# First attention's keys projected two heads at once and doubled by transfers within SBUF, the experts' gate kept in PSUM, the second sequence loaded later, in a kernel of two decoder blocks

## What is computed

```
# block 0, attention: 8 heads of 64; keys and values from the 512 tokens and 77 context rows
q = ln @ Wq ; k, v = split(concat([ctx_norm, ln]) @ Wkv)      # 589 keys
attn = softmax(8 * q @ k.T) ; x = x + tanh(g) * (attn @ v) @ Wout
# block 0, feed-forward: activations in 8 bit steps, ternary weights
h = silu(depthwise_conv1d(bit_linear(norm(x), w1))) ; x = x + tanh(g) * bit_linear(h, w2)
# block 1, attention: 16 heads of 8 against the 77 context rows, rotary positions
# block 1, feed-forward: 8 experts of 64, 2 chosen, and one shared expert
s = softmax(x @ gate_w.T) ; y = sum over chosen e of s_e * (silu(x @ wg_e) * (x @ wu_e)) @ wd_e
```

## Time and profile before

| | before |
|---|---|
| median of three runs | 289.64 us (289.44 to 291.3) |
| profiled execution: its time, its span | 291.28 us, 289.3 us |
| TensorE busy | 265.5 us, 92% |
| VectorE busy | 230.0 us, 79% |
| ScalarE busy | 172.6 us, 60% |
| GpSimd busy | 40.6 us, 14% |
| granted TensorE clock, mean share of full speed | 0.994 |

### The profile page before, as it was taken

One profiled execution on the slowest core, in us unless ns is written; L12 is line 12 of the kernel. 1 busy time (PEld: TensorE's weight loads), 2 busy tenths in 40 slices (PEclk: granted clock), 3 DMA queues, 4 the chain that ended last, 5 costly groups with the idle time before them and its releaser, 6 DMA issues.

```text
span 289.3 us, 5593 instructions
## 1 busy us (share of the span) xinstructions
PE 265.5 (92%) x1918; PEld 198.5 (69%) x1918; DVE 230.0 (79%) x545; ACT 172.6 (60%) x344; POOL 40.6 (14%) x60
## 2 busy tenths in 40 slices
PE   0999999999999999988899999999989868889796
PEld 0757877788789875667666678777657755575565
DVE  3698768796679998999898989758789989885751
ACT  1378856576775678587576659664357622752152
POOL 2200000000010000103100001003532030000650
PEclk9999999999999999999999999999999999999899
DMA  7950000000000000000000000000000100000001
GB/s 198 345 184 3 0 1 2 0 2 0 2 1 3 0 0 2 0 3 0 0 3 0 2 2 1 2 0 2 1 11 0 29 0 0 2 2 1 0 2 36
DMA packets 5856, 6.13 MB, mean 21 GB/s; under 512 B 555, under 2 KB 4805, under 8 KB 5829
## 3 DMA queue, kind: packets, MB, share of 16 engines
q1 hardware_dynamic: 4944, 4.66, 5.2%
q10 hardware_dynamic: 885, 1.12, 1.1%
HBM read 5.26 MB, written 0.52 MB: 20 GB/s over the span
## 4 chain that ended last, share of the span: by engine, by line
PE 68%; DVE 15%; issue 9%; ACT 4%; DMA 1%; POOL 1%; DVEq 0%; ACTq 0%; POOLq 0%
PE slot L510 19%; PE slot L583 12%; PE slot L564 6%; PE slot L565 5%; PE slot L555 3%; PE slot L556 3%; PE slot L548 2%; PE slot L542 2%; PE slot L677 2%; DVE mx L1095 2%; PE slot L590 2%; PE slot L643 2%; PE slot L655 2%; PE slot L726 1%; PE slot L660 1%
## 5 line engine op out<-in xcount | busy, mean ns | idle before, releaser
L804 ACT ACTIVATE PR<-slot,nm 128x589 f32<-128x589 f32 x64 | 47.5, 749 | 22.2 <-DVE nm L992 21.9
L992 DVE TENSOR_REDUCE nm<-slot 128x1 f32<-128x589 f32 x64 | 46.2, 762 | 4.2 <-PE slot L565 4.0
L510 PE MATMUL slot<-K,PR 128*128 128x128 f32 (+1 forms) x320 | 43.1, 276 | 0.4 <-ACT PR L804 0.4
L510 PEld LDWEIGHTS slot<-K,PR 128*128 128x128 f32 (+1 forms) x320 | 35.9, 142 | 8.1 <-ACT PR L804 4.4
L564 PE MATMUL slot<-KH,Q 128*128 128x296 f32 (+1 forms) x128 | 40.2, 332 | 0.1
L583 PE MATMUL slot<-PT,V 128*64 128x256 f32 (+1 forms) x320 | 38.1, 384 | 0.0
L565 PE MATMUL slot<-KL,Q 128*128 128x296 f32 (+1 forms) x128 | 36.1, 299 | 0.0
L741 ACT ACTIVATE PT<-slot 128x640 f32<-128x640 f32 x39 | 26.8, 704 | 12.6 <-PE slot L510 12.2
L583 PEld LDWEIGHTS slot<-PT,V 128*64 128x64 f32 (+1 forms) x320 | 21.6, 137 | 11.9 <-issue 2.7
L564 PEld LDWEIGHTS slot<-KH,Q 128*128 128x128 f32 x128 | 24.1, 189 | 3.5 <-issue 1.7
L565 PEld LDWEIGHTS slot<-KL,Q 128*128 128x128 f32 x128 | 24.2, 189 | 0.5 <-issue 0.5
(11 more groups left out here) (163 smaller groups left out, 516.2 us busy)
## 6 DMA issues: line engine op xcount, KB each, us to landing
CTT<-in_ctxT SPq DMA_DIRECT2D x1, 640.0 KB, 8.3
K<-in_const ACTq DMA_DIRECT2D x1, 589.0 KB, 8.9
WGU<-in_wgu SPq DMA_DIRECT2D x1, 580.0 KB, 8.5
X<-in_x SPq DMA_DIRECT2D x2, 256.0 KB, 3.9
WK<-in_wk SPq DMA_DIRECT2D x1, 512.0 KB, 6.5
out<-X SPq DMA_DIRECT2D x8, 64.0 KB, 1.5
L1W<-in_l1w SPq DMA_DIRECT2D x1, 384.0 KB, 8.4
WD<-in_wdT SPq DMA_DIRECT2D x1, 320.0 KB, 9.7
```

Source lines behind the costliest of these rows:

```text
L510: return pe.transpose(dst, src, ident[0:p, 0:p])
L804: act.activation(PR[:, s, :], W[:, K0:K0 + KEYS0], ACT.Exp, bias=nm0[:, s:s + 1], accum_out=sum0[:, b, p * 2 + f, t, e:e + 1]).then_inc(pr ...
L992: dve.tensor_reduce(nm0[:, s:s + 1], W[:, K0:K0 + KEYS0], AX.X, ALU.max, negate=True).then_inc(max_ready, 1)
```

## The change

1. A `k` item now holds a **pair** of heads: 8 items instead of 16, with the same two matmuls each. The product has one head on rows 0 to 63 and the other on rows 64 to 127. ScalarE and VectorE write `KH` and `KL` in two instructions of 64 rows each. SyncE then copies each 64 rows to the other half of the rows, four transfers for a pair (151 KB each), and a score item waits for `k_doubled`. `WK` is half as large (256 KB instead of 512): of each pair's four copies of 64 columns the two middle ones are loaded.
2. The experts' gate: ScalarE writes the tanh to PSUM, over the up product that it had copied; VectorE computes `(tanh + 1) * HM` once GpSimd has multiplied `HM`, and in an added stage `D2` multiplies by the gate product in PSUM. GpSimd's second multiplication (L503) is gone, and with it the waits that came of `HB` sharing memory with `TH`. The bank is held one stage longer.
3. The second half of `x` is loaded after `WK` and `WV`; its statistics and normalisation become stages of `x0` with places in the plan.
4. The plan is another one: other banks and another interleaving. More copies go to ScalarE: of the 64 copies behind `u` 45 instead of 39, of the 8 behind `f3` 7 instead of 4.

```diff
-        out += [("k", b, h) for h in range(H0)]
+        out += [("k", b, p) for p in range(NP0)]
...
 PLAN = """
-x0:F0 x0:A1 k:F2+8@2 k:F4 x0:D2 k:A1 k:F0 k:A1 k:D1 q:F6 k:D1 k:A1 q:F7 s:D2 q:A1 v:F2 k:D1 q:A1 q:D1 v:F4
+x0:F0 x0:A1 k:F2+8@2 x0:D2 q:F4 k:A1 v:F0 q:A1 s:D2 x0:P2 k:F6 v:Ca k:D1 q:F5 k:A1 q:D1 q:F0 q:A1 v:F2 k:D1
...
-        WK = sb("WK", [P, H0, P])
+        WK = sb("WK", [P, NP0, P])
...
+        k_doubled = [sem(f"k_doubled{i}") for i in range(2)]
...
-                    "m3": (shared_ready, n), "m2": (hid_ready, n), "m4": (y_ready, n)}[item[0]]
+                    "m3": (shared_ready, n), "m2": (hidw_ready, n), "m4": (y_ready, n)}[item[0]]
...
-            for b in range(B):
-                sp.dma_start(X[:, b * QT:(b + 1) * QT, :], xv[:, b * QT:(b + 1) * QT, :]).then_inc(ld[f"x{b}"], 16)
-            sp.dma_start(WK[:], wk.rearrange("p (h c) -> p h c", h=H0)).then_inc(ld["wk"], 16)
+            sp.dma_start(X[:, 0:QT, :], xv[:, 0:QT, :]).then_inc(ld["x0"], 16)
+
+            pairs = wk.rearrange("p (q c) -> p q c", q=NP0)[:, :, DH0:DH0 + P]
+            sp.dma_start(WK[:], pairs).then_inc(ld["wk"], 16)
             sp.dma_start(WV[:], wv).then_inc(ld["wv"], 16)
+            sp.dma_start(X[:, QT:, :], xv[:, QT:, :]).then_inc(ld["x1"], 16)
...
+            for g in range(B * NP0):
+                for part, signal in ((KH, k_upper), (KL, k_ready)):
+                    sp.wait_ge(signal, 2 * (g + 1))
+                    for e in range(2):
+                        r, o = slice(e * DH0, (e + 1) * DH0), slice((1 - e) * DH0, (2 - e) * DH0)
+                        s = (2 * g + e) % 4
+                        sp.dma_start(part[o, s, :].bitcast(F32), part[r, s, :].bitcast(F32)).then_inc(k_doubled[g % 2], 16)
...
-                    pe.wait_ge(k_ready, g + 1)
+                    pe.wait_ge(k_doubled[g // 2 % 2], 64 * (g // 4 + 1))
...
-                    act.activation(KH[:, g % 4, :], W[:, K0:K0 + KEVEN], ACT.Copy).then_inc(k_upper, 1)
+                    for e in range(2):
+                        r = slice(e * DH0, (e + 1) * DH0)
+                        act.activation(KH[r, (2 * g + e) % 4, :], W[r, K0:K0 + KEVEN], ACT.Copy).then_inc(k_upper, 1)
...
-                    dve.tensor_tensor(KL[:, (n - 1) % 4, :], W[:, K0:K0 + KEVEN], KH[:, (n - 1) % 4, :].bitcast(F32),
-                                      ALU.subtract).then_inc(k_ready, 1)
+                    for e in range(2):
+                        dve.wait_ge(k_upper, 2 * n - 1 + e)
+                        r, s = slice(e * DH0, (e + 1) * DH0), (2 * (n - 1) + e) % 4
+                        dve.tensor_tensor(KL[r, s, :], W[r, K0:K0 + KEVEN], KH[r, s, :].bitcast(F32),
+                                          ALU.subtract).then_inc(k_ready, 1)
...
-                    act.activation(HB[:, (n - 1) % 2, :], slot(item)[:, 0:MH], ACT.Tanh, scale=0.5).then_inc(gate_tanh, 1)
+                    act.wait_ge(up_copied, n)
+                    act.activation(W[:, MH:2 * MH], W[:, 0:MH], ACT.Tanh, scale=0.5).then_inc(gate_tanh, 1)
...
-                    hb = HB[:, (n - 1) % 2, :]
-                    dve.scalar_tensor_tensor(out=hb, in0=hb, scalar=1.0, in1=W[:, 0:MH],
+                    dve.wait_ge(upw_ready, n)
+                    hm = HM[:, (n - 1) % QT, 0:MH]
+                    dve.scalar_tensor_tensor(out=hm, in0=W[:, MH:2 * MH], scalar=1.0, in1=hm,
                                              op0=ALU.add, op1=ALU.mult).then_inc(hid_ready, 1)
...
+                elif kind == "m2":
+                    dve.wait_ge(hid_ready, n)
+                    hm = HM[:, (n - 1) % QT, 0:MH]
+                    dve.tensor_tensor(hm, hm, W[:, 0:MH], ALU.mult).then_inc(hidw_ready, 1)
```

More of the change, by code:

```diff
@@ L154, in takes @@
     kind, n = item[0], item[-1]
-    return {"x0 D2": n == 0, "f4 P2": n % TP == TP - 1, "f4 D3": n % TP == TP - 1}.get(f"{kind} {stage}", True)
+    return {"x0 D2": n == 1, "x0 P2": n == 1, "x0 D3": n == 1, "f4 P2": n % TP == TP - 1, "f4 D3": n % TP == TP - 1}.get(f"{kind} {stage}", True)
 def orders():
@@ L249, in mega_kernel @@
         rt = sb("rt", [P, NT, 4])
[L250 removed]
+        hot = sb("hot", [P, TP, 2, E1])
         cwt = sb("cwt", [P, NT, E1])
@@ L494, in power @@
                 n = upto(item)
-                rstd(*{"n": (1, n - 1, PARTS), "f4": (2, n // TP - 1, PARTS), "a6": (3, n - 1, PARTS)}[item[0]])
-            def halves(item):
-                n = upto(item)
-                pool.wait_ge(hid_ready, n)
-                pool.wait_ge(upw_ready, n)
-                hm = HM[:, (n - 1) % QT, 0:MH]
-                pool.tensor_tensor(hm, hm, HB[:, (n - 1) % 2, :], ALU.mult).then_inc(hidw_ready, 1)
-            walk("POOL", {"P1": work, "P2": power, "P3": halves})
+                rstd(*{"x0": (0, 1), "n": (1, n - 1, PARTS), "f4": (2, n // TP - 1, PARTS), "a6": (3, n - 1, PARTS)}[item[0]])
+            walk("POOL", {"P1": work, "P2": power})
         @block.tensor
@@ L549, in front @@
                 elif kind == "k":
-                    h = item[2]
+                    p = item[2]
                     pe.wait_ge(lt_ready, 2 * (b + 1))
@@ L960, in _ @@
                                   ALU.subtract, ALU.mult).then_inc(cn_ready, 1)
-            dve.wait_ge(ld["x1"], 16)
-            all_stats(0, X, slice(QT, NT))
-            variance(0, slice(QT, NT), twice=True)
             def early(item):
@@ L1129, in second @@
                 if kind == "x0":
-                    dve.wait_ge(rstd_ready[0], 2)
-                    for m in range(QT, NT):
-                        normalise(0, X, m, XN[:, m, :], xn_ready[0])
-                    dve.wait_ge(ld["ident"], 16)
-                    dve.tensor_copy(identb[:], ident).then_inc(identb_ready, 1)
+                    dve.wait_ge(ld["x1"], 16)
+                    all_stats(0, X, slice(QT, NT))
+                    variance(0, slice(QT, NT), twice=True)
                 elif kind == "s":
@@ L1200, in third @@
                 kind, n = item[0], upto(item)
-                if kind == "n":
+                if kind == "x0":
+                    dve.wait_ge(rstd_ready[0], 2)
+                    for m in range(QT, NT):
+                        normalise(0, X, m, XN[:, m, :], xn_ready[0])
+                    dve.wait_ge(ld["ident"], 16)
+                    dve.tensor_copy(identb[:], ident).then_inc(identb_ready, 1)
+                elif kind == "n":
                     dve.wait_ge(rstd_ready[1], n)
```

116 lines of the change are left out of this document (52 added, 64 removed).

## The result

The changed kernel takes 286.76 us (median of four runs, 285.93 to 287.35) against 289.54 for the one before (289.05 to 291.3): a ratio of 0.9891, 95% interval 0.9843 to 0.994. It is faster by 1.1%, which is clear of the noise; I had forecast 283, 2.3%, so it is 3.8 us short of the forecast. The profiled execution took 286.67 us, its span is 284.9.

What follows compares the result with a forecast made beforehand. TensorE was taken to bound the first 40 scores, VectorE the next 16, no engine the later chains. Stretches 21.4 + 81.7 + 56.5 + 105 + 18.5 = 283.1 us, plus 2.0 less 1.6: 283.5, written 283; own range 279 to 287, with rivals 276 to 291.

Steps and rivals of the forecast that it cites:

- TensorE bounds it, so TensorE work taken out of B is time: First to 40th score maximum: TensorE busy 82.8 of 83.2 us, so less TensorE work there shortens the kernel.
- B: Stretch from the first to the 40th score maximum; forecast 81.7 us for 83.2, at least 79.5.
- The first doubling's queue: Pair 1's key transfers wait behind SyncE's loads, ending about 18 us; landing at about 20, at worst 21 us.
- A: Start to the first score maximum: loads, first normalisation and projections; forecast 21.4 us for 20.5, at most 22.5.
- Rival 3: Doublings late, a pair's last transfer over 5 us from a loaded queue; +3 to +4 us, time 287; chance 0.10.
- −1.6: Final step: median of three runs lay 1.64 us below the profiled execution, so 1.6 us is subtracted.
- E: Last normalised rows to the end, the last experts; forecast 18.5 us for 17.2, range 16.5 to 20.
- D: 64th score maximum to last normalised rows; forecast 105 us for 75.4, VectorE busy 94.5 us times ratio 1.11.
- Rival 1: VectorE stays fed behind the last score, ratio 1.087, and TensorE's cut shows in full; time 276; chance 0.15.
- C: Stretch from the 40th to the 64th score maximum; forecast 56.5 us for 93.0, range 54 to 60.
- Load of the second sequence: At the start, moving this load from the queue's head gains nothing, since the first sequence's chain never waited behind it.
- Normalisations under 400 ns: Sign in the changed profile: the normalisations' mean, 452 ns before, falls under 400 ns with fewer GpSimd multiplications.

Runs made afterwards that it cites:

- e18: Kernel before, old order, with four more filling transposes ahead of each of the sixteen key items, 64 in all; 295.84 us, ratio 1.0197.
- e5: e1's kernel with nine filling transposes ahead of each of the eight key items, putting the key products' time back; 293.4 us, ratio 1.0066.
- e9: Kernel before, old order, with the eight odd heads' key products in bfloat16, rougher output; 290.75 us, ratio 1.0003.
- e13: e8's kernel with all eight pairs' key products in bfloat16, rougher output; 281.49 us, ratio 0.9702.
- e17: e8's kernel with maxima over every second column and key products in bfloat16, only times used; 277.75 us, ratio 0.9554.
- e16: e8's kernel with each score's maximum over every second column and exponential's scale 0.8, another output; 280.22 us, ratio 0.9635.
- e2: Kernel before, old order, with the key part alone (pairs of heads, doubling by transfers); 304.47 us, ratio 1.0445.
- e12: e2's kernel with the five late loads moved behind the first two pairs' doublings; 298.47 us, ratio 1.0281.
- e8: e1's kernel with fourteen more filling transposes behind the second a6 item's back stage; 282.13 us, ratio 0.9741.
- e1: Changed kernel with five late weight loads issued behind the transfers that double the first two pairs of keys; 284.45 us, ratio 0.9809.
- e15: e8's kernel with each pair's two steps of doublings held back on SyncE by a small load and its wait; 287.2 us, ratio 0.9911.
- e4: Changed kernel with GpSimd's second multiplication back in place of VectorE's added stage; 289.41 us, ratio 0.9975.
- e11: Changed kernel with only the fourteen filling transposes behind the second a6 item, loads where they were; 284.25 us, ratio 0.9798.
- e6: e1's kernel with the third pair's query copy on ScalarE placed behind the three exponentials of its group; 287.72 us, ratio 0.9914.
- e7: e1's kernel with 7 of the 28 ScalarE copies behind the first 40 scores given back to VectorE; 284.32 us, ratio 0.9867.
- e10: e8's kernel with the second half of x loaded ahead of the key and value weights again; 281.95 us, ratio 0.9711.

## Why the prediction was wrong

- **"TensorE bounds it, so TensorE work taken out of B is time": the step that failed.** It was read from 82.8 busy of 83.2 us. A full engine shows that more of its work will cost (e18 6.3 of 6.7 us, e5 7.5 of 7.5), not that less will gain (between the 1st and the 64th maximum: e9 nothing of 3.4 us, e13 0.4 of 4.3, or 1.1 without its fallen clock, e17 beside e16 1.5 of 4.3). The key part alone lengthens the old order by 15 us, 9 with the queue out of the way (e2, e12). Yet in the new order putting the key time back costs 7.6 us, e5 against e8: 288.4 us of span against 280.8. With its key time put back the new order (288.4) is no better than the old one (287.3 at full clock). So in these runs neither the order nor the saved time gains by itself; only the new plan together with the saved time does. B's term was 4.0 us too small: 0.8 of it more busy time, 3.2 idle. My sum had taken 1.5 us of items off B's old length one for one, as if the new order would leave TensorE as little idle as the old one (0.4 us); it idles 3.6, of which 2.3 are for ScalarE's exponentials and 1.2 for copies by VectorE and ScalarE.
- **The first doubling's queue was named, and mis-sized.** I let the loads end near 18 us, from a window of before, and put the worst landing at 21. In the changed kernel the DMA share is 1.08 from 18 to 20 us and the landing was 21.8. e1 gives the price: 2.3 us of time; A's term was 1.4 too small. The 2.5 us for an unhindered transfer held, and the two thin places, pairs 1 and 3, were the right ones (e15). Rival 3 had them late for a loaded queue, and gave 287; it happened for pair 1.
- **The step from the sum to the median, "−1.6".** The profiled execution of before had a mean clock of 0.994; the fall from 272.3 us on lies in its E. Such executions take about 2.2 us more than those at 1.00. I took its span as the base and its distance to the median as a constant. After, the distance between span and time was 1.8 and the median was the profiled one: the −1.6 had no counterpart.
- **D: VectorE's work about right, the ratio too high, and its meaning not shown.** VectorE was 92.4 busy (94.5 forecast). The ratio was 1.075, for 1.11; with the clock up it is 1.05 (e8, 96.7 us for 92.0 busy). VectorE busy was 93%, as "over 88%" asked. But D's length did not follow VectorE's work: e4 takes 2.1 us off it, with 5.0 more on GpSimd, and D stays; e8 leaves it as it is, and D falls by 2.6. Rival 1 had a low ratio in D, and lost it in A and B. That the span came within 1.8 us of the sum is luck: D's −5.7 stands against the +4.0 of B and the rest.
- **What I had not named: the clock.** In the changed kernel all four executions have 0.970 to 0.982, with D's fall in the profiled one. e11 prices it at 2.5 us. What makes it fall in one execution and not in another (e5, e6, e7) is open.
- **C** came out at 57.5 for 56.5. **E** at 19.6 for 18.5, within its 16.5 to 20, but the 17.2 it started from held the fallen clock: against the 15.9 of e18 E grew by 3.7 us, where I had 1.3. **Load of the second sequence** counted at nothing: right (e10). **64 rows cost as 128**: right, 768 ns for 768. **Normalisations under 400 ns: wrong**, 491. GpSimd's first multiplication stays, and two normalisations beside it still take 2.05 us. The second multiplication was worth 2.6 us (e4), more than the 1 us I took, and in E, not in D where I took it. (The Trainium skill, SBUF — State Buffer, SBUF: two separate sides, has the port pair that VectorE and GpSimd share held for a whole instruction. These 2.05 us agree with it, and no run here took the two apart.)

Together: without the queue and without the fall of the clock the change would be worth 7.4 us (e8: 282.13 for 289.54), more than forecast; 2.1 to 2.3 went to the queue and 2.3 to 2.5 to the clock.

## What to carry to other kernels

In this case a busy share near 100% told what more work costs; what less work gains had to be shown by making it less, in the order that will be used, since the order and the saving were worth nothing apart. Before summing from one profiled execution, look at its mean granted clock beside that of the other runs: a fall inside a stretch is part of its length there. The same holds for a run that is to settle something: e13's small gain held a fall behind a new wait. Small transfers that something waits for do not belong behind loads that nothing waits for yet.
